# Cross attention of a decoder layer: the next context's remainder waits for the rectified tile's remainder

## The reference

```python
x = x + xattn(layernorm(x), ctx_2048, ...)
def xattn(input1, input2, ...):             # input1: normed x, input2: context, both [16, 256, 512]
    theta_x = einsum('ld,bdt->btl', theta_w, input2) + theta_b
    phi_x = einsum('ld,bdt->blt', phi_w, input1) + phi_b[:, None]
    p = softmax(einsum('btl,bls->bts', theta_x, phi_x), axis=-1)      # 512 x 512 per batch row
    g_x = einsum('ld,bdt->btl', g_w, input1) + g_b
    t_x = einsum('bts,bsl->blt', p, g_x)
    mu, var = mean(t_x, (1, 2)), var(t_x, (1, 2))
    h = relu((t_x - mu) * rsqrt(var + 1e-5) * ln_gamma + ln_beta)
    return einsum('ol,blt->bot', out_w, h) + out_b[None, :, None] + input2
```

## Time and profile before

| | |
|---|---|
| median of 3 runs | 3150.95 us (3143.74 to 3153.2) |
| the profiled execution, its own time | 3147.36 us |
| its span in the trace | 3145.7 us |
| mean granted TensorE clock over the span | 0.949 |
| cross attention in the trace | from about 774 to about 1180 us |

### The profile page before, as it was taken

How to read it: one execution, slowest core, us unless ns; L and a number is a source line. 1 busy time by engine, 2 the same in 40 slices (tenths; PEclk the granted TensorE clock), 3 DMA queues, 4 the chain that set the end, 5 groups by cost and what they waited for, 6 DMA issues and landing times.

```text
span 3145.7 us, 46652 instructions
## 1 busy us (share of the span) xinstructions
PE 2806.4 (89%) x16538; PEld 2355.5 (75%) x16538; DVE 1324.7 (42%) x2260; ACT 886.9 (28%) x1637; POOL 867.1 (28%) x1208
## 2 busy tenths in 40 slices
PE   7979999948878770399999999999999999999998
PEld 6855555336666660399999999999999999999997
DVE  6756777436888884112313313213213223223211
ACT  2126666612445441112212212212112112112110
POOL 4546777513232225501201101201111110210210
PEclk9999999869998985699999999999999999999999
DMA  3102222222121213202303203203213212112110
GB/s 101 40 3 40 46 45 45 50 71 77 54 79 41 80 54 85 82 14 91 97 13 101 92 11 108 87 21 108 71 36 102 67 61 84 61 64 84 40 47 20
DMA packets 97028, 194.68 MB, mean 62 GB/s; under 512 B 22030, under 2 KB 23726, under 8 KB 96752
## 3 DMA queue, kind: packets, MB, share of 16 engines
q1 hardware_dynamic: 75072, 131.85, 14.4%
q0 software_dynamic: 21808, 60.65, 6.2%
HBM read 148.77 MB, written 38.94 MB: 60 GB/s over the span
## 4 chain that ended last, share of the span: by engine, by line
PE 58%; issue 2%; DMA 1%; DVE 0%; POOL 0%; ACT 0%; SPq 0%; DVEq 0%; POOLq 0%
PE ex_hid L1730 29%; PE ex_acc L102 9%; PE ex_acc L103 9%; PE ex_acc L104 9%; PE ex_xb L1700 1%; DMA ex_raw<-in_w_tiles_dram 1%; DVE ex_w_l L1632 0%; DVE ex_w_l L1635 0%; ACT ex_w_h L1601 0%; DMA ex_ys<-xn_dram,ex_rows_in 0%; POOL out_dram L1582 0%; DMA ex_ys<-slot_table_dram 0%; SPq L1528 0%; ACT ex_w_h L1603 0%; DVE ex_ys L1643 0%
## 5 line engine op out<-in xcount | busy, mean ns | idle before, releaser
L1651 DVE SCALAR_TENSOR_TENSOR ex_h0l<-ex_hid,ex_h0h 128x640 fp32r<-128x640 f32 x128 | 105.6, 825 | 689.9 <-ACT ex_h0h L1610 682.9
L1651 DVE SCALAR_TENSOR_TENSOR ex_h1l<-ex_hid,ex_h1h 128x640 fp32r<-128x640 f32 x128 | 105.6, 825 | 612.8 <-ACT ex_h1h L1610 578.5
L1610 ACT ACTIVATE ex_h0h<-ex_hid 128x640 fp32r<-128x640 f32 x128 | 90.3, 705 | 738.3 <-PE ex_hid L1730 725.9
L592 DVE TENSOR_REDUCE at_nb<-at_ring 128x2 f32<-128x512 f32 (+1 forms) x384 | 246.9, 686 | 121.8 <-PE at_ring L664 121.7
L1610 ACT ACTIVATE ex_h1h<-ex_hid 128x640 fp32r<-128x640 f32 x128 | 90.3, 705 | 736.7 <-PE ex_hid L1730 708.6
L1546 POOL COPY ex_gi<-ex_slot_gather 128x1 int32 (+1 forms) x84 | 16.2, 193 | 899.3 <-PE ex_xb L1700 890.6
L102 PE MATMUL ex_acc<-ex_w_h,ex_h1h 128*128 128x512 f32 x640 | 254.5, 398 | 0.0
L102 PE MATMUL ex_acc<-ex_w_h,ex_h0h 128*128 128x512 f32 x640 | 253.1, 395 | 0.0
L103 PE MATMUL ex_acc<-ex_w_l,ex_h0h 128*128 128x512 f32 x640 | 250.5, 391 | 0.0
L103 PE MATMUL ex_acc<-ex_w_l,ex_h1h 128*128 128x512 f32 x640 | 250.4, 391 | 0.0
L104 PE MATMUL ex_acc<-ex_w_h,ex_h1l 128*128 128x512 f32 x640 | 249.8, 390 | 0.0
(11 more groups left out here) (271 smaller groups left out, 5998.6 us busy)
## 6 DMA issues: line engine op xcount, KB each, us to landing
ex_raw<-in_w_tiles_dram SPq DMA_DIRECT2D x256, 256.0 KB
x_in<-in_x_dram SPq DMA_DIRECT2D x32, 256.0 KB
act<-at_raw SPq DMA_DIRECT2D x128, 64.0 KB
at_recb<-o_rec_dram SPq DMA_DIRECT2D x16, 512.0 KB
op_x<-in_x_dram SPq DMA_DIRECT2D x32, 256.0 KB
cx_ctx<-in_ctx_dram SPq DMA_DIRECT2D x16, 512.0 KB
out_dram<-cx_res SPq DMA_DIRECT2D x16, 512.0 KB
xn_dram<-cx_prob SPq DMA_DIRECT2D x16, 512.0 KB
```

The costliest lines, as they stand in the source:

```text
L592: dve.tensor_reduce(nb[e][:, r, p % 2, heads, qb], bank(e, f"s{n}")[:].rearrange("p (h k) -> p h k", h=heads.stop - heads.start), AX.X, AL ...
L1610: act.activation(h[f % 2][0][:], hid[:, :, 0:HB], ACT.Relu).then_inc(sm["h_hi"], 1)
L1651: dve.scalar_tensor_tensor(h[f % 2][1][:], hid[:, :, 0:HB], 0.0, f32(h[f % 2][0][:]), ALU.max, ALU.subtract).then_inc(sm["h_lo"], 1)
```

## The change

Pool's instruction stream gets one more wait in the tail of each step but the last. Behind the two roots of the variance and ahead of the two `ctx_lo` subtractions it now waits until `h_lo` of both chains of this step is done (`h_lo` counts one per chain, so the value is 2j + 2). Everything that stands behind it in Pool's order stands behind this wait too. No instruction changes its place in the order of its engine, no data and no other wait change. All lines behind L978 move down by one.

```diff
                     pool.tensor_tensor(grstd[:, c:c + 1], gve[:, c:c + 1], t["half"][:], ALU.pow)\
                         .then_inc(sm["grstd"], 1)
                 if ahead:
+                    wait_apart(pool, sm["h_lo"], CB * j + CB, sm["passed_pool"])
                     front(j + 1)
                 for c in chains:
                     n = CB * j + c
```

## The result

| | before | after |
|---|---|---|
| median of 12 runs each | 3148.37 us | 3140.96 us |
| lowest and highest | 3143.74 to 3153.2 | 3136.79 to 3147.3 |
| span of the profiled execution | 3145.7 us | 3135.8 us |
| cross attention in the trace, first L1074 to last logits | 408.5 us | 401.6 us |

The ratio of the two is 0.9979, with a 95% interval from 0.9969 to 0.9988: 0.21% less, some 6.6 us. It is taken over all runs, so it differs a little from the quotient of the medians, which lie 7.4 us apart. The gain is less than the 0.3% that the prediction took as the bound of a change that shows, lies within the range given (3138 to 3155), and is twice the 3.0 us of the forecast's sum. The cross attention alone became 6.9 us shorter in the profiled execution.

A forecast was written before the change was run, and what follows sets the result against it. PE bounds the cross attention's tail where phi is slow, DVE's L1177 where it is fast. 5 x 0 + 1.51 + 1.46 = 3.0 us less, from a median of 3150.95 to 3148.0 us; range 3138 to 3155.

The forecast's parts named there:

- the forecast's sum: Total over seven cross-attention steps: nothing in five, 1.51 and 1.46 us in two, 3.0 us less.
- The held time and its removal: DVE's L1170 and L1177 are held by Pool's L960, 2.92 us a step; the wait removes this in seven steps.
- Zero in the steps with a slow phi: Five steps with phi at 1.2 GHz: L1094 waits for g's high part anyway, so the change is worth 0.
- 1.5 us in a step with a fast phi: Fourth and sixth steps, phi at 2.4 GHz: L1094 of chain 1 can start 1.51 and 1.46 us earlier.
- what the rule would add: Closing PE's 1.1 us gap could keep the clock up, 1.64 us in the router: 6.3 us instead of 3.0.
- 2 of 7: Two steps had phi at 2.4 GHz and PE waiting 1.1 us for L1177; the other five were counted at 0.
- The row shows the two together and not that one makes the other: Reason for leaving out 1.64 us: PE's wait for L1177 and slow router matmuls stood in the same steps.
- the gap ahead of phi: PE's gap before phi, left alone by the change; phi ran slowly after it in five steps.
- the rival that counted each fast phi as 1.5 us gained: Clock turns out better: all seven phis fast, 10.4 us; with other slow stretches gone 16.5, 3134.5 us; chance 0.15.
- All of the holding on the path: Rival: all of DVE's held time in seven steps counts, 20.4 us less, 3130.6 us; chance 0.03.
- The holding moves to L1094 and L1186: Rival: Pool in its new place holds these DVE instructions, 12.6 us slower, 3163.5 us; chance 0.05.
- Theta doesn't wait for L960: Pool's later end costs PE's theta nothing: margin at least 1.2 us, just in time in the sixth step.

The follow-up runs named there:

- wait_first_h_lo: The changed kernel with Pool's wait on h_lo of chain 0 only, not of both chains: 3140.84 us, ratio 0.9971.
- gap_after: The changed kernel, in which PE also waits for both g remainders ahead of the output projection: 3163.76 us, ratio 1.0047.
- the new order: Output projection ahead of g of chain 1 on PE, that remainder behind the statistics on DVE: changed kernel 3122.53 us, kernel before 3152.04 us.
- wait_scaled: The changed kernel with Pool's wait on the two scaled tiles (L1171) in place of h_lo: 3164.58 us, ratio 1.0033.
- half_g_after: The changed kernel with half of g's matmuls left out in every front: 3125.45 us, ratio 0.9918.
- half_g_before: The kernel before with half of g's matmuls left out in every front: 3152.01 us, ratio 1.0009.

## Why the prediction was right, and what was mis-sized

**The held time and its removal: right.** L1171 went from 3.54 to 1.41 us a pair and L1178 from 2.15 to 1.29, in all seven steps. Pool waits 3.8 to 4.1 us for `h_lo`, as worked out.

**Zero in the steps with a slow phi: right.** The changed kernel has one such step left, its first. There L1095 of chain 1 waits 1.99 us for ACT, and the step is 49.38 us; the kernel before has 49.39 for its third, which had the same slow phi and slow transposes in front of the next one. wait_first_h_lo has two more steps with a slow phi: 47.93 and 49.49 us, where the kernel before has 47.93 and 49.39. The two kernels with half of g show that g's matmuls are what hid the held time.

```profile
826.07 0.69 DVE L1095 TENSOR_TENSOR cx_r<-cx_bank,cx_r 128x512 fp32r<-128x512 f32 x1 [0.59 <-ACT cx_r L1016]
828.75 0.69 DVE L1095 TENSOR_TENSOR cx_r<-cx_bank,cx_r 128x512 fp32r<-128x512 f32 x1 [1.99 <-ACT cx_r L1016]
```

**1.5 us in a step with a fast phi: right. What was mis-sized is the clock, which the sum put at nothing.** The two steps that had a fast phi before gained what was worked out: the residual starts 7.8 to 7.9 us behind L1165, where it had started 9.37 behind L1164. That is the 3.0 us of the sum. But these two steps also had the slow router, and with the wait for L1177 it went: 2 x 1.64 = 3.3 us. This is the term that the prediction gave as what the rule would add and left out; with it the sum is 6.3, and 6.6 were measured.

The count of "2 of 7" was wrong as well, but it cost nothing. Four more steps have a fast phi after the change, so their residual starts 1.6 us earlier (7.8 to 7.9 and not 9.46). The same four have the slow transposes ahead, 1.6 us each: 4 x 1.6 gained, 4 x 1.6 given back. The trace has 6.9 us less over the stage; the 0.6 above 6.3 isn't traced to anything. Part of the forecast's 7.0 us of error (3148.0 against 3140.96) isn't of the kernel: it was set against a median of three runs, 2.6 us above that of twelve.

**The clock.** "The row shows the two together and not that one makes the other" was the right caution, and gap_after now shows that the gap makes the slow router, in this order of the work. By the Trainium skill ("TensorE: Matmul & The Clock Gate", section "What's actually happening") the throttled state is the default and activity releases it. The trace agrees for the router: no gap of 1.1 us, and both slow routers are gone, 3.3 us. It doesn't tell when phi is fast. The prediction took the gap ahead of phi as what keeps it slow; that wait of PE for L1148 (L1149) is 2.1 us ahead of every phi of both kernels, the fast and the slow. What goes with a fast phi is what PE did further ahead, in the softmax's transposes. So the rival that counted each fast phi as 1.5 us gained, and seven of them as 10.4, left out their price.

**The rivals.** All of the holding on the path: not here. Half of g or the new order puts most of it there: without the wait the residual starts 13.8 and 15.6 us later over the seven steps, of the 20.4 that were held. The holding moves to L1094 and L1186: no; under Pool they take 0.69 and 2.72 us as before. That it moves to another instruction can happen all the same, and wait_scaled shows its price, 3.5 us a step. Theta doesn't wait for L960 in the changed kernel, but the margin is thin: chain 1's theta starts 0.23 to 0.28 us behind Pool's end in the six steps with a fast phi. In half_g_after PE does wait for L960, up to 0.7 us in every step.

**Left open.** What decides in a given step whether the pair is slow transposes and a fast phi, or the other way round, I can't tell from these runs. One profiled execution each doesn't show how often a pattern comes back, and the runs of one kernel differ by 10 us and more.

## What to carry to other kernels

Before time that an engine loses is called a gain, find the next point at which it meets another engine, and read who comes last there: here 20 us of held time were worth 7, since PE's matmuls covered most of it, and 26 to 30 us as soon as the cover was cut or moved, roughly half of it through the clock behind the gap. Look then at the order of the engine that has become the cover: with the wait in place, moving one block of matmuls behind the work that DVE needs was worth another 17 us. A gap in TensorE's work can be paid twice, once as a wait and once in the clock of the matmuls behind it, so a change that opens one can eat all that it saves (half_g_before left out 19 us of matmuls for nothing). And when one stretch of matmuls has become fast, look for one that has become slow before the first is counted as gained.

## What was not expected of the hardware

DVE instructions with two inputs in SBUF and Pool's subtraction held each other in both directions, and the one that had started finished. L1170 takes 2.88 us in place of 0.75 when it starts behind Pool, and Pool's second subtraction, behind that L1170, takes 2.83 in place of 2.41. With Pool's two instructions in a row, each of two DVE instructions can meet one of them: 4.85 us for a pair that takes 1.29. With DVE first, as in wait_first_h_lo, DVE loses nothing and Pool's first subtraction takes 2.49 us in place of 2.39.

The time of the softmax's transposes and of phi together hardly changes: 6.6 + 3.0 us in one step, 5.0 + 4.5 or 4.3 + 5.5 in another, 9.5 to 9.9 in all of the 77 tails but one (8.7). A gap of 1.5 us ahead of the output projection and theta came with a router at 1.2 GHz in seven steps of seven, though these matmuls themselves, 5.7 us of them, ran at 2.4 GHz in six of the seven.
